# Token preparation inside the pipeline's last steps, and the last node's list loaded at once

## What is computed

```
x = x + conv(ln_c(x))
t = tokens(x)
n = ln_t(t)
h = (n @ W_gat).reshape(M, HEADS, NUM_EXPERTS)
a_src = (h * att_src).sum(-1)
a_dst = (h * att_dst).sum(-1)
e = leaky_relu(a_src[src] + a_dst[dst])
alpha = softmax of e over the edges of one dst, self loops included
agg = segment_sum(h[src] * alpha) + b_gat
scores = layernorm(agg).mean over heads, best two, softmax
out = sum over experts of gate * (gelu(n @ W1 + b1) @ W2 + b2)
x = t + out
```

## Time and profile before

| | us |
|---|---|
| median of 3 runs | 4371.58 |
| lowest, highest | 4370.59, 4375.14 |
| the profiled execution | 4372.52 |
| its span | 4370.6 |
| token block, first load to the next block's first DMA | 2294.5 to 2427.4 |
| rounds, first gather to the last round's append | 2450.0 to 4135.5 |

### The profile page before, as it was taken

The page is one execution under the profiler, slowest core; times in us unless marked ns, Lnnn a source line. Parts: engine busy times, 40 slices in busy tenths (PEclk is TensorE's granted clock), DMA queues, the critical chain, the costliest instruction groups (busy, mean ns, idle before and its releaser), DMA issues. The chain is left out here.

```text
span 4370.6 us, 30088 instructions
## 1 busy us (share of the span) xinstructions
PE 2945.5 (67%) x9220; PEld 1503.4 (34%) x9220; DVE 2992.9 (68%) x4591; ACT 1543.8 (35%) x2216; POOL 1333.0 (30%) x1388
## 2 busy tenths in 40 slices
PE   6888897999999998898757235535544553554019
PEld 2333343444444443343227113322322232232019
DVE  8999668787888786976744546645654664664575
ACT  2222235444545443545425023223222322332117
POOL 0000000000000000000003577777777777777600
PEclk8888998999999999999875567766776776776559
DMA  4211322454545454545757212112111211111637
GB/s 153 78 58 53 111 92 79 136 172 140 178 150 168 153 158 152 182 148 170 257 185 237 28 35 46 37 37 49 42 37 44 47 37 38 34 18 17 23 130 287
DMA packets 342679, 458.36 MB, mean 105 GB/s; under 512 B 83156, under 2 KB 257110, under 8 KB 333688
## 3 DMA queue, kind: packets, MB, share of 16 engines
q1 hardware_dynamic: 296760, 416.46, 29.5%
q0 software_dynamic: 45760, 40.00, 7.0%
HBM read 342.80 MB, written 113.51 MB: 104 GB/s over the span
## 5 line engine op out<-in xcount | busy, mean ns | idle before, releaser
L1457 POOL DMA_INDIRECT got<-scratch_tab,src_at x1280 | 1222.8, 955 | 390.0 <-issue 378.4
L595 PE MATMUL in_ps<-xT,w_in 128*128 128x512 f32 x2048 | 938.6, 611 | 6.2 <-issue 6.2
L1404 PE MATMUL hid_ps<-tokens,w 128*128 128x512 f32 x512 | 318.1, 754 | 858.5 <-ACT hid L1623 838.3
L554 POOL MEMSET w_in<- 1x128 int32 x1 | 0.2, 194 | 2039.2 <-PE in_ps L595 2039.2
L595 PEld LDWEIGHTS in_ps<-xT,w_in 128*128 128x128 f32 x2048 | 394.8, 197 | 486.6 <-issue 486.6
L612 PE MATMUL out_ps<-w_out,act 128*128 128x512 f32 x1024 | 477.8, 612 | 65.2 <-issue 36.9
L907 DVE TENSOR_TENSOR keys<-keys 128x1024 f32<-128x1024 f32 x380 | 464.4, 1222 | 10.7 <-ACT keys L721 9.6
L908 DVE TENSOR_TENSOR keys<-keys 128x1024 f32<-128x1024 f32 x380 | 464.2, 1222 | 0.0
L1552 DVE TENSOR_TENSOR hold<-by_value,is_loop 128x256 f32<-128x256 f32 x20 | 8.5, 425 | 632.3 <-ACT by_value L1634 632.3
L1404 PEld LDWEIGHTS hid_ps<-tokens,w 128*128 128x128 f32 x512 | 109.7, 238 | 954.0 <-ACT hid L1623 848.1
L1634 ACT ACTIVATE by_value<-got 128x1536 f32<-128x1536 f32 x20 | 80.5, 4027 | 772.4 <-DMA got<-scratch_tab,src_at 772.4
(11 more groups left out here) (267 smaller groups left out, 4069.9 us busy)
## 6 DMA issues: line engine op xcount, KB each, us to landing
w_out<-in_m_WoutT SPq DMA_DIRECT2D x256, 512.0 KB, 4.6
w_in<-in_m_WinT SPq DMA_DIRECT2D x128, 512.0 KB, 4.0
scratch_y<-ys SPq DMA_DIRECT2D x25, 1024.0 KB, 4.0
got<-scratch_tab,src_at POOLq DMA_INDIRECT x1280
xT<-scratch_xt SPq DMA_DIRECT2D x8, 2048.0 KB, 9.9
scratch_sz<-zst SPq DMA_DIRECT2D x64, 256.0 KB, 5.0
gz<-scratch_sz SPq DMA_DIRECT2D x64, 256.0 KB, 5.1
tokens<-scratch_y SPq DMA_DIRECT2D x16, 1024.0 KB, 8.9
```

What stands on the lines that cost most here:

```text
L595: last = t_.matmul(in_ps[:, z, :], w_in[:, n % WIN, k, :], xT[:, s % 2, k, :], start=(k == 0), stop=(k == KC - 1))
L1404: last = t.matmul(hid_ps[:, f], w1[:, e, f * P:(f + 1) * P], tokens[:, g * QW:(g + 1) * QW], start=True, stop=True)
L1457: g.indirect_dma_start(got[:, y, t, :], None, tab_d[:, :], bass.IndirectOffsetOnAxis(ap=src_at[:, y, t:t + 1], axis=0))\
```

## The change

The token block goes away as a block of its own. Its work is done in steps 66 to 83 of the pipeline: `tokens_turn(b)`, `tokens_first(b)`, `tokens_root(b)`, `tokens_second(b)` and `tokens_normal(b)` in step `b + 66`, `tokens_back`, `tokens_copy` and `table_part` in the step behind it, `table_rows(b)` one later and `store_rows(b)` one later still. It uses the pipeline's own tiles: `in_ps` for the first transposes and `turn_ps` for the ones back, in two halves, and for the table product, each of them single. The loads of `x` and `v`, the sum, and the store of `x2` are all GpSimd's. The last four images are not stored as `v` but added where they stand (`DIRECT`). The keys and `xT` lie in what becomes the token tile. The row search begins six steps earlier and reads its rows in two portions. The first 19 pieces of the last node's list are loaded in one DMA (`load_first_last`) at the start of the rounds, with `load_keys` moved ahead of most memsets; only the loop's rounds call `load_last`. The count works on half as many elements at a time. The first block's semaphores are cleared at the end of the third.

```diff
+SEARCH = KC * (NI - 1) + 4
+TOK_AT = KC * NI + 2
+DIRECT = B - 4
+STEPS = TOK_AT + B + 2
+FIRST_LAST = (2 * PAIRS + 1) * FR
+PADS = -(-FIRST_LAST // P)
...
+                def load_tokens(b):
+                    if b < B:
+                        if b >= 3:
+                            g.wait_ge(s_tt, b - 2)
+                            g.wait_ge(s_x2[b % 3], 16 * (b // 3))
+                        g.dma_start(xw[b % 3], x_in[b]).then_inc(s_xw[b % 3], 16)
+                        if b < DIRECT:
+                            if b >= 2:
+                                g.wait_ge(s_add, b - 1)
+                            g.wait_ge(s_vst[b % 2], 16 * (b // 2 + 1))
+                            g.dma_start(xv[b % 2], v_d[b]).then_inc(s_xv[b % 2], 16)
...
+                for b in range(B):
+                    g.wait_ge(s_xw[b % 3], 16 * (b // 3 + 1))
+                    if b < DIRECT:
+                        g.wait_ge(s_xv[b % 2], 16 * (b // 2 + 1))
+                    else:
+                        g.wait_ge(s_v, b + 1)
+                    g.tensor_tensor(xw[b % 3], xv[b % 2] if b < DIRECT else xo[b % 2], xw[b % 3], ALU.add).then_inc(s_add, 1)
+                    g.wait_ge(s_add, b + 1)
+                    g.dma_start(x2_d[b], xw[b % 3]).then_inc(s_x2[b % 3], 16)
+                    load_tokens(b + 2)
...
+                def tokens_turn(b):
+                    if 0 <= b < B:
+                        t_.wait_ge(s_add, b + 1)
+                        if b:
+                            t_.wait_ge(s_norm, b)
+                        for k in range(KC):
+                            last = t_.transpose(tok_ps[:, k, :], xw[b % 3][:, k * P:(k + 1) * P], ident[:])
+                        last.then_inc(s_tt, 1)
+                def tokens_back(b, half):
+                    if 0 <= b < B:
+                        t_.wait_ge(s_norm, b + 1)
+                        if half:
+                            t_.wait_ge(s_tk, 2 * b + 1)
+                        elif b:
+                            t_.wait_ge(s_row, b)
+                def table_part(b):
+                    if 0 <= b < B:
+                        t_.wait_ge(s_tk, 2 * b + 2)
...
                     turned((t, 3))
                     root((t, 1))
+                    tokens_root(t - TOK_AT)
+                    tokens_copy(t - TOK_AT - 1, 0)
...
                     turned((t, 6))
+                    tokens_normal(t - TOK_AT)
+                    tokens_copy(t - TOK_AT - 1, 1)
...
                     tick((t, 0))
+                    table_rows(t - TOK_AT - 2)
+                    tokens_first(t - TOK_AT)
                     scan(t - SCAN_AT - 1)
+                    tokens_second(t - TOK_AT)
...
+                    if t == SEARCH + 2:
+                        v.wait_ge(s_rows, 32)
+                        rows_before(0)
+                        v.sem_inc(s_rowi, 1)
+                        rows_before(1)
...
+                load_keys()
+                load_first_last()
...
-                        load_last(1 - y)
+                        if not first:
+                            load_last(1 - y)
```

More of the change, by code:

```diff
@@ L230, in program @@
                  for m in (1, 2)]
-            keys = [sb(f"keys{n}", [P, KF], F32, st) for n in range(2)]
-            xT = sb("xT", [P, 2, KC, QW], F32, st)
+            keys = [tokens[:, n * KF:(n + 1) * KF] for n in range(2)]
+            xT = tokens[:, 2 * KF:].rearrange("p (x k n) -> p x k n", x=2, k=KC)
             act = sb("act", [P, 3, KC, QW], F32, st)
@@ L344, in program @@
             s_v = first_sem("s_v")
+            s_xv = [sem("s_xv0"), sem("s_xv1")]
+            s_xw = [sem(f"s_xw{n}") for n in range(3)]
+            s_x2 = [sem(f"s_x2{n}") for n in range(3)]
+            s_add = first_sem("s_add")
+            s_tt = first_sem("s_tt")
+            s_tw = first_sem("s_tw")
+            s_wt = first_sem("s_wt")
+            s_tch = first_sem("s_tch")
+            s_tst = first_sem("s_tst")
+            s_tsd = first_sem("s_tsd")
+            s_tsh = first_sem("s_tsh")
+            s_norm = first_sem("s_norm")
+            s_bk = first_sem("s_bk")
+            s_tk = first_sem("s_tk")
+            s_h = first_sem("s_h")
+            s_row = first_sem("s_row")
+            s_tab = [first_sem(f"s_tab{n}") for n in range(4)]
+            s_rnd = first_sem("s_rnd")
             s_vst = [first_sem("s_vst0"), first_sem("s_vst1")]
@@ L414, in load_image, with store_rows @@
                         sp.dma_start(xin[b % 2], x_in[b]).then_inc(s_px[b % 2], 16)
+                def store_rows(b):
+                    if 0 <= b < B:
+                        sp.wait_ge(s_row, b + 1)
+                        with nc.allow_non_contiguous_dma(reason="a row of the table to a node"):
+                            sp.dma_start(tab_d[b * S:(b + 1) * S, :].rearrange("(t p) f -> p t f", p=P),
+                                         rows[:, b % 4]).then_inc(s_tab[b % 4], 16)
                 def load_parameters():
@@ L1074, in _ @@
                     norms((t, 4))
-                    if t == search:
+                    if t == SEARCH:
                         v.wait_ge(s_first, 32)
@@ L1394, in _ @@
                 sp.wait_ge(s_mw, 96)
+                for used in first_sems:
+                    sp.sem_clear(used)
             @block.tensor
```

451 lines of the change are left out of this document (198 added, 253 removed).

## The result

The changed kernel takes **4335.4 us** (median of 4 runs, 4332.4 to 4341.3) against 4371.4 of the kernel before on the same chip (4 runs, 4370.6 to 4375.1). The ratio is 0.991, with a 95% interval of 0.990 to 0.993: 36 us less, clear of the noise. The forecast was 4339, in a range of 4300 to 4374, and its mechanism was the likeliest one.

The account below looks back on a forecast made before the run. GpSimd's issue rate bounds the rounds, TensorE the pipeline up to step 63, then a ScalarE-VectorE chain. Terms -3.4, +1.5, -10.2 and -21.3 sum to -33.4 us, giving 4339, range 4300 to 4374.

Parts of the forecast that it names:

- Part 1: Fixed rounds: 18 loads of b_k on GpSimd go away, 17 x 1.25 = 21.3 us less; bounds 0 and 18 x 1.30.
- Rival (d): Rounds: the 18 removed loads bring nothing because the gathers' transfers are the limit, 4360; inside the forecast's 0.70.
- Part 2: Opening of the rounds: key load issued before the memsets, first gather at 12.4 us, 10.2 less; bounds 6 and 12.
- Part 3: Row search moved to steps 60 to 66: scan of step 65 ends at 2086 instead of 2071.6, 14.4 us later.
- Part 4: Tokens in steps 66 to 81: 133 us block removed, three waits lengthen steps; rounds' block begins at 2424 against 2427.4.
- Step 72: Pipeline step after 67 to 71: without output units on TensorE it was to take 21.0 us.
- Steps 74 to 78: Steps without a scan: TensorE is the bound, 17.3 us each, five of them 86.5.
- rival (b): Steps 74 to 79: TensorE's units run at 1.2 GHz, 29 us a step instead of 17.3, 4397; chance 0.12.
- Rival (a): Steps coupled less: 21 us for steps 67 to 71, 15 for 74 to 78, about 4299; chance 0.07.
- Rival (c): Handovers and waits add up to 2 us a step more, 32 over 16 steps: 4371, no change; chance 0.11.
- GpSimd's own part: Token work on GpSimd: 3 DMAs and an add, under 6 us an image, hidden; 1.5 us for adds delaying VectorE.
- Rival (e): GpSimd's loads and stores slowed beside VectorE: no more than 1 us, or 8 at 3 us a DMA, 4347; inside 0.70.

## Why the prediction was right, point by point

**Part 1, the last node's list.** Forecast -21.3, measured -20.0. The 18 intervals between the first 19 appends are 1501.0 us instead of 1521.6, -20.6, and the run with the load kept has them back. The 1.3 us that are missing are in the gathers (956 against 955 ns each); VectorE's additional work is not shown to be their cause, for on C the same work goes with 955 ns and 1499.4 to 1499.8 us. Rival (d), that the loads bring nothing, falls on the first chip and on C; on A and B, where something else lengthens the rounds, its outcome is what was seen within their noise.

**Part 2, the opening.** Forecast 12.4 us, -10.2; measured 14.9, -7.7. The largest miss is the landing. By the rows it is 0.8 to the first load, 6.7 from its issue to its use (5.5 forecast: "1 less since the queue is quieter" was wrong), 6.1 for the merge with its handover (5.4 forecast; its first instruction is held up by a fill, 1.10 us against 0.30) and 1.3 for one load. The forecast's own addends also make 12.75, not the 12.4 it carried; and its total, 4371.6 less 33.4, makes 4338.2 and not 4339.

**Part 3, the row search.** Forecast: the scan of step 65 ends at 2086; measured 2086.95. Errors cancel. TensorE waited 0.9 us for w_out in all where 4 were put; VectorE's scan of step 65 was 2.4 us longer through GpSimd's add, and a product of step 64 1.6 us (2.24 instead of 0.69), which had been priced elsewhere; the rest, 10.5 us, is the 10.4 of the forecast. The run with the search a step sooner says as well that it isn't fully hidden where it stands.

**Part 4, the long steps.** In us:

| steps | forecast | measured |
|---|---|---|
| 66 | 30.8 | 30.7 |
| 67 to 71 | 127.5 | 122.0 |
| 72 | 21.0 | 29.8 |
| 73 | 19.3 | 20.6 |
| 74 to 78 | 86.5 | 75.6 |
| 79 | 12.7 | 13.8 |
| to the rounds' block | 40 | 39.6 |

The coupling was read rightly: softplus waits for dt_part in these steps (rows above), and taking either of the two named waits away shortens them. Steps 67 to 71 are 24.4 us each and not 25.5: the small products run at the high clock in part of them (turn to dt_part 6.0 us in step 68, where 7.5 were summed). Step 67, whose first two units are at the low clock (5.74 us), takes 26.0, and the same step on B, where they take 4.08, 23.8. Step 69, 26.5 us, is no matter of the clock: it has the wait of step 72, below. **Step 72** was the one wrong by its reasoning and not its size. "Step 72 has no units: 21.0" took something away from TensorE, which isn't what ends last there; the copy of the table's rows behind the output's normalisation does, a fourth wait that the forecast's "three waits tie them together" did not have. The edit on the rows' place shows it for 4.5 of the 8.8 us; most of the others are VectorE's normalisation of an output image, for which the forecast had no term. **Steps 74 to 78** went the other way. Here is one of them, TensorE:

```profile
2322.25 1.07 PE L748 MATMUL in_ps<-ident,w_in 128*128 128x128 f32 x8
2323.16 3.60 PE L704 MATMUL out_ps<-w_out,act 128*128 128x512 f32 x8
...
2336.04 1.07 PE L748 MATMUL in_ps<-ident,w_in 128*128 128x128 f32 x8
```

Every record of this step is at the high clock; the window 2285 to 2365 has it granted at 0.94. 13.8 us, under the 14.9 of "all fast", and 15.1 in the mean where 17.3 were taken. With that **rival (b)**, the slow kernel through TensorE's clock at 1.2 GHz (29 us a step, 4397), falls: with TensorE busy 75 of 80 us the small products between the units didn't bring the clock down. It is where TensorE waits that L748 takes 1.95 us and not 1.07: at the heads of steps 72 to 74, with 13 of 40 us busy from 2240 to 2280 and a granted clock of 0.50. **Rival (a)**, the loose coupling, has steps 74 to 78 right (15) and steps 67 to 71 wrong (21, against 24.4). **Rival (c)** falls with both.

**GpSimd's own part.** The forecast put 1.5 us for adds that collide with VectorE. Three of the collisions, 2.4 us at step 65, 2.1 in step 69 and 2.2 in step 72, stand in chains that others wait for, and there are others of 1.3 to 1.6 us whose share on the path was not measured. By these rows it should have been some 6 us, an estimate, since no run took the adds away. The Trainium skill, SBUF — State Buffer, section "Who interferes with whom", has the rule for a VectorE instruction with two inputs in SBUF, and the trace agrees: the scan (3.58 us instead of 1.20) is one of them.

**Rival (e)**, GpSimd's DMAs held up beside VectorE, exists and is small. GpSimd's load of the third row and its store of image 0, and VectorE's compare in the row search beside the store:

```profile
2032.60 2.99 POOL L620 DMA_INDIRECT tokens<-scratch_sorted,row_i  x1 [51.62 <-DVEq L1284]
...
2052.75 2.64 POOL L650 DMA_DIRECT2D scratch_x<-w_in  x1 [0.30 <-POOL w_in L648]
...
2052.93 2.34 DVE L1175 TENSOR_SCALAR tokens<-tokens,bin_key 128x4096 f32<-128x4096 f32 x1
```

The store's issue takes 2.64 us and ends with the compare; the median of the 16 is 0.57. The row load takes 2.99 us beside another compare of this size (2032.43, 2.35 us), where those of the first two rows took 1.13 and 1.81. So VectorE's kind of work does matter, and these two issues are the ones that the compares held up. "GpSimd's own part is 3 DMAs at about 1 us" was too dear: 0.54, 0.53 and 0.57.

**The end.** The 2.0 us behind the last append of the rounds were not forecast. 1.2 of them lie before the append after it; of the other 0.8 no cause was looked for, and the stretch from the last append of the rounds on varies by 1.2 us between the four kernels on C.

So 38.1 us gained against 33.4 forecast is made of 2.0 (end), 5.5 (steps 67 to 71) and 10.9 (steps 74 to 78) that came on top, and 2.5 (opening), 1.3 (rounds), 8.8 (step 72) and 1.3 (step 73) that came short; the other terms cancel to 0.2. The mechanism holds: 27.7 of the 38.1 us are parts 1 and 2, and nearly all of the removed block came back as longer steps. That the total is within 5 us is luck in part, since errors of 8.8 and 10.9 us stand against each other in it.

Of the signs that the prediction named, b_k loads down from 21 to 2 and softplus released by dt_part came true, and a round of 83.3 us was near the 83.0; the first gather came 14.9 us into its block and not 12 to 13, and the last store of the tables was issued at 2416 and not near 2421.

## What to carry to other kernels

Where work is moved into an in-order pipeline, list for each engine what stands behind the waiting instruction, also the short copies that another engine waits for: the two cheapest edits here, a few lines of TensorE's and ScalarE's order, gave nearly as much as the whole change (32.4 us at the first gather). When a step is a ring over three engines, taking one wait away can make the next one longer, as it did here, so try edits in pairs before dropping one. And an engine that only issues DMAs is priced by its issue time: the load of 19 pieces at once took GpSimd 0.96 us to issue, that of one piece 0.94 to 1.03.

## What the runs showed of the hardware

- **Two of the chips starve the rounds.** On A and B a fixed round takes 115 to 128 us (the first interval 106 to 108) instead of 83.3, though GpSimd issues its gathers as fast as elsewhere (0.94 us and 0.30). While the list runs, TensorE, ScalarE and VectorE run one instruction every 1 to 3 us, mostly with no semaphore to wait for. TensorE on A:

```profile
3027.37 3.78 PE L1437 MATMUL hid_ps<-tokens,w 128*128 128x512 f32 x4 [33.37 <-issue]
...
3038.64 0.37 PE L1453 MATMUL y_ps<-w,hid 128*128 128x128 f32 x1 [2.43 <-issue]
```

  Windows on B during the list, and after its end, columns as above:

```profile
3020.00:3040.00 20.00, 0.00 (x0) 0.00 (x0) 0.00 (x0) 1.15 (x2) 15.12 (x17) 0.50 0.11 10
...
3080.00:3100.00 20.00, 15.74 (x63) 9.65 (x62) 17.36 (x27) 9.79 (x11) 0.00 (x0) 0.84 0.02 10
```

  Once GpSimd pauses, the others run at their usual pace. The pipeline ahead of the rounds is not touched. That the instructions themselves are brought late, by transfers that stand behind GpSimd's, is a guess from the releaser "issue"; no run tested it, and what sets these two chips apart is not known.
- **A VectorE instruction beside an add of GpSimd can last until the add ends.** From 1.20 to 3.58 us for a scan, 1.22 to 3.40 for a 128x1024 product, 0.69 to 1.98 for a 128x512 one.
- **A compare of 128x4096 on VectorE holds up a DMA that GpSimd issues:** from 0.57 to 2.64 us for a direct one, from 1.13 to 2.99 for an indirect one.
- **Direct DMAs are cheap for GpSimd to issue,** 0.53 to 0.58 us, against 0.94 to 1.03 for the indirect ones in the rounds, with 0.30 us between two of those and none between a direct one and the next.
